# Three column parts of the layer-0 edge sums beside the experts, pauses in the column scans, two expert reloads behind the end rows

## The reference

```
x = x + gnn0(ln(x)) + mix0(ln(x))
x = x + ffn0(ln(x))       # the part that is changed
x = x + gnn1(ln(x), edges) + mix1(ln(x));  x = x + ffn1(ln(x))

ffn0: h = x @ W_gat                                  # 4 heads x 4 experts
      e = leaky_relu(a_src[src] + a_dst[dst])        # per edge and head
      alpha = softmax of e over the edges of each dst
      scores = layernorm(segment_sum(h[src]*alpha)).mean(heads); top 2, softmax -> gate
      out = sum over 4 experts: gate[e] * (gelu(x@W1[e]+b1[e]) @ W2[e] + b2[e])
```

## Time and profile before

| | |
|---|---|
| median of the runs | 4406.01 us |
| the profiled execution: its own time / its span | 4400.95 / 4399.2 us |
| busy PE, DVE, ACT, POOL | 2388.0, 1799.8, 1362.5, 1277.8 us |
| experts end / layer-1 sort begins (VectorE) | 2053.6 / 2100.4 us |
| sort ends / last sums end | 2404.6 / 2440.2 us |
| end rows there / gates begin / combine begins | 2487.2 / 2502.0 / 2516.8 us |

### The profile page before, as it was taken

How to read it: one execution, slowest core, us unless ns; L and a number is a source line. 1 busy time by engine, 2 the same in 40 slices (tenths; PEclk the granted TensorE clock), 3 DMA queues, 4 the chain that set the end, 5 groups by cost and what they waited for, 6 DMA issues and landing times. The chain is left out here.

```text
span 4399.2 us, 45890 instructions
## 1 busy us (share of the span) xinstructions
PE 2388.0 (54%) x14500; PEld 1769.9 (40%) x14500; DVE 1799.8 (41%) x3887; ACT 1362.5 (31%) x3051; POOL 1277.8 (29%) x1238
## 2 busy tenths in 40 slices
PE   3677455634111110896475126434535466899997
PEld 2532324533000110664352125333434354688885
DVE  6898355770000000113899674434434366111112
ACT  2479235631000000111268001434434332122221
POOL 0000040005777776000000215545344421500005
PEclk9999676765555555998599568667767676999998
DMA  1210112003111111111130213434333320354553
GB/s 62 93 37 0 46 32 79 0 1 60 22 13 12 9 11 11 34 33 41 60 118 39 74 36 78 156 98 149 112 126 136 97 89 21 107 188 188 186 188 93
DMA packets 165531, 322.54 MB, mean 73 GB/s; under 512 B 71298, under 2 KB 126592, under 8 KB 156845
## 3 DMA queue, kind: packets, MB, share of 16 engines
q0 software_dynamic: 62656, 149.60, 12.2%
q1 hardware_dynamic: 102753, 171.54, 11.5%
HBM read 213.40 MB, written 107.37 MB: 73 GB/s over the span
## 5 line engine op out<-in xcount | busy, mean ns | idle before, releaser
L1645 POOL DMA_INDIRECT ge_near<-gat_src,s_other x512 | 516.4, 1009 | 171.9 <-issue 171.9
L1947 PE MATMUL bank<-arena 128*125 128x256 f32 x800 | 219.9, 438 | 627.6 <-issue 582.8
L2752 POOL DMA_INDIRECT he_buf<-wh_dram,s_other x400 | 387.0, 967 | 404.3 <-DVEq L2986 283.5
L1947 PEld LDWEIGHTS bank<-arena 128*125 128x125 f32 x800 | 170.5, 218 | 683.9 <-issue 622.5
L1974 DVE TENSOR_TENSOR XN<-bank,arena 125x256 f32 (+1 forms) x100 | 42.4, 425 | 984.2 <-remote 580.1
L1960 ACT ACTIVATE arena<-bank,arena 128x500 f32<-128x500 f32 (+1 forms) x112 | 70.6, 633 | 957.8 <-DMA q_gb<-in_L_mix_bn_beta_cols 657.7
L2872 ACT ACTIVATE he_buf<-he_buf,he_e 128x128 f32<-128x128 f32 x800 | 239.4, 387 | 36.8 <-issue 34.4
L2432 ACT ACTIVATE x_hT<-bank,x_w 128x256 f32<-128x256 f32 x256 | 121.4, 474 | 379.4 <-PE bank L2384 379.4
L2393 PE MATMUL bank<-x_w,x_hT 128*128 128x256 f32 x1024 | 229.4, 382 | 6.9 <-ACT x_hT L2432 6.7
L2384 PE MATMUL bank<-x_xT,x_w 128*128 128x256 f32 x1024 | 228.1, 381 | 0.9 <-DVE x_xT L2187 0.9
L2393 PEld LDWEIGHTS bank<-x_w,x_hT 128*128 128x128 f32 x1024 | 191.9, 190 | 39.3 <-issue 13.2
(11 more groups left out here) (696 smaller groups left out, 5989.9 us busy)
## 6 DMA issues: line engine op xcount, KB each, us to landing
he_result<-he_buf SPq DMA_DIRECT2D x25, 2080.0 KB
XN<-s_a_dram SPq DMA_DIRECT2D x57, 512.0 KB
x_y<-XN SPq DMA_DIRECT2D x24, 500.0 KB
x_x<-zero SPq DMA_DIRECT2D x1, 8192.0 KB, 27.0
ge_near<-gat_src,s_other POOLq DMA_INDIRECT x512
x_xs<-x_x SPq DMA_DIRECT2D x32, 256.0 KB, 3.4
x_y<-x_ys SPq DMA_DIRECT2D x32, 256.0 KB, 2.1
he_buf<-wh_dram,s_other POOLq DMA_INDIRECT x400
```

The lines of the kernel that those rows point to most:

```text
L1645: pool.indirect_dma_start(out=G[:, c, 0:HF + H], out_offset=None, in_=m.gat_src, in_offset=bass.IndirectOffsetOnAxis(ap=ed.other[:, c:c + ...
L1947: last = pe.matmul(m.ps[4 + j % 2][:P, 0:D], self.hT[:, f, j * P:(j + 1) * P], w.w2[e][:, f, :], start=f == 0, stop=f == FC - 1)
L2752: pool.indirect_dma_start(out=buf[j][:, c, 0:HF + H], out_offset=None, in_=m.wh_dram, in_offset=bass.IndirectOffsetOnAxis(ap=ed.other[:, t ...
```

## The change

The parts become 0-128, 128-192, 192-384 and 384-512 columns. Parts 0 and 1 (192 columns) are done between the chunks of experts 2 and 3, whose loops on VectorE and ScalarE are written out; `s.spread` moves ahead of expert 2. Behind the sort come parts 2 and 3, with one `dec` of 192 columns in place of two halves of 128. The scans of both sorts are drained after every fourth. The wait for the sort and `reload(3)` leave SP's order; the small block with `reload(0)` goes; both reloads are issued by SP within `join_nodes` when the end rows have landed.

```diff
@@ Sort.vector_scan
         for i in range(KB):
             dve.tensor_tensor_scan(H3[:, 1:, i], ...)
-        dve.drain()
+            if i % 4 == 3:
+                dve.drain()
@@ join_nodes(..., then=None)
+            if then is not None:
+                @block.sync
+                def _(sp):
+                    sp.wait_ge(rows[NG - 1], 16 * GT)
+                    then(sp)
@@ gat_edges
-            dec = m.sb("ge_dec", [128, 2 * CQ, H])
+            PARTS = ((0, 128), (128, 192), (192, 384), (384, 512))
+            dec = m.sb("ge_dec", [128, 192, H])
+            dec_of = lambda q: dec[:, 0:PARTS[q][1] - PARTS[q][0], :]
@@ sync
                     s1.sync(sp)
                     sp.wait_ge(s1.negated, 1)
                     ex.reload(sp, 1)
                     ex.reload(sp, 2)
-                    sp.wait_ge(sorted1, 1)
-                    ex.reload(sp, 3)
                     keep(2)
                     keep(3)
@@ vector: logits(q) is split into scores(q) (L1665, L1667) and maxima(q) (the rest),
@@         sums(q) into weigh(q) (L1689, L1692) and sums(q, heads) (L1696)
+                    def beside(q):
+                        def between(dve, c):
+                            if c == 0:
+                                scores(q)
+                            elif c == 1:
+                                maxima(q)
+                            elif c == 2:
+                                weigh(q)
+                            elif c == 3:
+                                sums(q, (0, 1))
+                            elif c == 4:
+                                sums(q, (2, 3))
+                        return between
                     s.positions(dve)
-                    for e in range(4):
-                        ex.vector(dve, e)
+                    ex.vector(dve, 0)
+                    ex.vector(dve, 1)
                     s.spread(dve)
                     dve.drain()
-                    logits(0)
-                    logits(1)
-                    sums(0)
-                    sums(1)
+                    ex.vector(dve, 2, beside(0))
+                    ex.vector(dve, 3, beside(1))
                     dve.wait_ge(ex.freed, 4 * (NCH + 1))
                     s1.vector(dve)
-                    dve.drain().then_inc(sorted1, 1)
-                    logits(2)
-                    logits(3)
-                    sums(2)
-                    sums(3)
+                    scores(2)
+                    maxima(2)
+                    scores(3)
+                    weigh(2)
+                    sums(2, range(H))
+                    maxima(3)
+                    weigh(3)
+                    sums(3, range(H))
@@ scalar
-                    for e in range(4):
-                        ex.scalar(act, e)
-                    weights(0)
-                    weights(1)
+                    ex.scalar(act, 0)
+                    ex.scalar(act, 1)
+                    ex.scalar(act, 2, beside(0))     # weights(q) after chunk 1
+                    ex.scalar(act, 3, beside(1))
@@ end of gat_edges
-        with nc.Block() as block:
-            @block.sync
-            def _(sp):
-                sp.wait_ge(r_stored, 64)
-                ex.reload(sp, 0)
+        def reload(sp):
+            ex.reload(sp, 3)
+            ex.reload(sp, 0)
         join_nodes(..., reload)
@@ Experts0.vector and .scalar (between=None)
-        chunks(dve, body)
+        if between is None:
+            chunks(dve, body)
+        else:
+            for c in range(NCH + 1):
+                body(c, 4 if c < NCH else 1)
+                between(dve, c)
```

More of the change, by code:

```diff
@@ L1356, in _, with join_nodes @@
                 s.spread(dve)
-def join_nodes(m, tag, ed, sp_, H, F, GT, last, result, r_stored, add_nodes, own_e=None, early=None, late=None):
+def join_nodes(m, tag, ed, sp_, H, F, GT, last, result, r_stored, add_nodes, own_e=None, early=None, late=None, then=None):
     nc, cols = m.nc, ed.cols
@@ L1658, in _, with scores @@
                     mx = G[:, :, HF + H:W]
-                    def logits(q):
-                        lo, hi = q * CQ, (q + 1) * CQ
+                    def scores(q):
+                        lo, hi = PARTS[q]
                         e = spread.ke[:, lo:hi, :]
+                        blocks_done = hi // BC
                         for j in range(2):
-                            dve.wait_ge(rows[j], 16 * BC * (hi // BC // 2))
+                            dve.wait_ge(rows[j], 16 * BC * ((blocks_done + 1 - j) // 2))
                         dve.tensor_tensor(e, G[:, lo:hi, HF:HF + H], e, ALU.add)
@@ L1668, in logits, with maxima @@
                         dve.drain()
+                    def maxima(q):
+                        lo, hi = PARTS[q]
+                        e, d = spread.ke[:, lo:hi, :], dec_of(q)
                         for h in range(H):
@@ L1680, in logits, with weigh, sums @@
                         dve.drain()
-                        wide = spread.cont[:, lo:hi].unsqueeze(2).broadcast_to((128, CQ, H))
+                        wide = spread.cont[:, lo:hi].unsqueeze(2).broadcast_to((128, hi - lo, H))
                         dve.tensor_tensor(d, d, wide, ALU.mult)
                         dve.drain().then_inc(e_ready, 1)
-                    def sums(q):
-                        lo, hi = q * CQ, (q + 1) * CQ
-                        e, d = spread.ke[:, lo:hi, :], dec[:, q % 2 * CQ:(q % 2 + 1) * CQ, :]
+                    def weigh(q):
+                        lo, hi = PARTS[q]
+                        e, d = spread.ke[:, lo:hi, :], dec_of(q)
                         dve.wait_ge(e_exp, q + 1)
-                        dve.tensor_tensor(d, d, spread.cont[:, lo:hi].unsqueeze(2).broadcast_to((128, CQ, H)), ALU.mult)
+                        dve.tensor_tensor(d, d, spread.cont[:, lo:hi].unsqueeze(2).broadcast_to((128, hi - lo, H)), ALU.mult)
                         for h in range(H):
                             f = G[:, lo:hi, h * F:(h + 1) * F]
-                            dve.tensor_tensor(f, f, e[:, :, h].unsqueeze(2).broadcast_to((128, CQ, F)), ALU.mult)
+                            dve.tensor_tensor(f, f, e[:, :, h].unsqueeze(2).broadcast_to((128, hi - lo, F)), ALU.mult)
                         dve.drain()
-                        for h in range(H):
+                    def sums(q, heads):
+                        lo, hi = PARTS[q]
+                        e, d = spread.ke[:, lo:hi, :], dec_of(q)
+                        for h in heads:
                             for f in (*range(h * F, (h + 1) * F), HF + h):
@@ L1697, in sums @@
                                                        G[:, lo - 1, f:f + 1] if q else 0.0, ALU.mult, ALU.add)
[L1698 removed]
+                        if H - 1 in heads:
+                            dve.drain().then_inc(summed, 1)
+                    def beside(q):
[11 more added lines that the diff above has]
+                        return between
                     dve.tensor_copy(dst_logits[:, :, :], m.hg[:, :, 20:24])
@@ L1950, in tensor, with scalar @@
         chunks(pe, body)
-    def scalar(self, act, e):
+    def scalar(self, act, e, between=None):
         m, w, FC = self.m, self.w, self.FC
@@ L1961, in body, with vector @@
                                bias=w.b1[e][:, f:f + 1]).then_inc(self.acted, 1)
-        chunks(act, body)
-    def vector(self, dve, e):
+        if between is None:
+            chunks(act, body)
+        else:
+            for c in range(NCH + 1):
+                body(c, 4 if c < NCH else 1)
+                between(act, c)
+    def vector(self, dve, e, between=None):
         m, w = self.m, self.w
```

20 lines of the change are left out of this document (11 added, 9 removed).

## The result

Twenty runs of each kernel give 4401.58 us before and 4423.35 us after (medians; 4389.03 to 4411.55 and 4401.60 to 4430.74). The ratio of the runs is 1.0042, with an interval of 1.0030 to 1.0054: slower by a little, 21.8 us by the medians and 18.5 us by the ratio (13 to 24). The profiled execution of the changed kernel has 4424.19 us, its span 4422.5 (before 4400.95 and 4399.2). The busy times hardly differ: VectorE 1799.7 us against 1799.8, TensorE 2387.9 against 2388.0. Hardly any work was added (four table loads on ScalarE, and the pauses); what changed is what waits for what.

The account below looks back on a forecast made before the run. No engine sets the whole time; each stage has its own chain, and what ends last there counts. +13.3 from the combine on and +1.1 for layer 0's scans, +14.4 on 4404.3, gave 4419 us; own range 4412 to 4426.

Parts of the forecast that it names:

- The two reloads, the step that decides: Behind the end rows: 51.1 us for both on five engines, gates' loads queued behind them, combine 13.3 us later.
- T: Moment when the end rows are there, before gates and combine; forecast to move by -24.35 us, to 2462.8.
- Start of the sort: Layer 1's sort on VectorE: starts 29.9 us sooner, at 2070.5, bounds 2067 to 2075.
- Work between the chunks: Around experts 2 and 3: fits VectorE's idle time, but ScalarE makes TensorE late; +2.5 us, bounds 0 and twice 4.5.
- Scans: Both sorts on VectorE: seven more drains each cost +1.1 us a sort, bounds 0 and 2.
- Parts 2 and 3: Behind layer 1's sort: 320 columns in place of 256 and two new waits, +7.2 us, bounds 5 and 10.
- Start of the join: First end-row gather: without the small block's barrier it starts at about 2445.1, -2.75 us, bounds -3 and 0.
- The sum: Whole kernel: +13.3 us from the combine on and +1.1 for layer 0's sort scans, +14.4.
- Small loads pass: Rival at the gates: engines take the loads between the reloads, combine at T + 51.5, -1.4 us, 4403; 7%.
- ScalarE's tables: Rival in the sort: a table load each of six rounds, 7.7 us more, 4427; 9% together with dearer work between chunks.
- Reloads hidden: Rival at the combine: both reloads land before T + 29.65, whole -24.35 us reaches the combine, 4381; 4%.
- The base: Starting time for the whole kernel: the mean of four executions, 4404.3 us, giving 4418.7, called 4419.

Follow-up runs that it names:

- e1: Changed kernel with reload(3) issued again when the sort is over and reload(0) once the keeps have landed; 3431.71 us, ratio 0.9997 to the kernel before.
- e3: Kernel before with only the reloads of experts 3 and 0 moved behind the end rows and the small block gone; 3463.84 us, ratio 1.0097.
- e7: Changed kernel with the gates' three loads issued by SP in the join ahead of the two late reloads; 3447.03 us, ratio 1.0039 to before.
- e4: Changed kernel with every reload, still late, cut in two DMAs of 112 and 13 partitions; 3439.7 us, ratio 1.0027 to the kernel before.
- e6: Changed kernel with early reloads, reloads and first load of X cut in 112 and 13 partitions, one drain a sort; 3413.0 us, ratio 0.9943 to before.
- e8: e6 with one call moved, scores(3) behind sums(2); 3415.58 us, ratio 0.9933 to the kernel before.
- e2: Changed kernel with the gates' three loads issued by ScalarE on its own queue, reloads still late; 3462.5 us, ratio 1.0086 to the kernel before.
- c_after: The changed kernel run again, no edit, on the chips of the experiments; 3459.46 us, ratio 1.0069 to the kernel before.
- c_before: The kernel before run again, no edit, one look on the chips of the experiments; 3428.8 us.

## Why the prediction was right, point by point

- **The two reloads, the step that decides.** Forecast 51.1 us for the pair, gates at T + 52.6 and a combine at T + 67.3; measured a wait of 41.27 us, gates at T + 51.1, combine at T + 65.9. The mechanism is shown from both sides (e1, e3), and the order on the queue by the DMA view above and e7. The rule of the Trainium skill that was drawn on (DMA: Bandwidth & Descriptors, Why a DMA increments its semaphore by 16 and not by 1) holds too: 112 partitions instead of 125 filled 16 engines in e4 and e6. The price of a packet rose as more engines ran.
- **Start of the sort.** Forecast 2070.5, measured 2070.15. The 0.35 is about what the last chunk came sooner than forecast: 2.1 us late and not 2.5 (next point).
- **Work between the chunks.** Forecast +2.5 us. From chunk 1 to chunk 2 of expert 2 it is 16.23 us, as rows 1892.94 and 1909.17 show, against 14.7 for expert 3 (1986.99 to 2001.71): +1.5 and 0; 0.5 were there before the first of the new work, and the last add is 2.1 us later than before. The sort feels this in full: SP issues the keeps (2060.17) only when the last chunk's store has landed, and the sort's loads behind them. ScalarE's timeline (below) has the two Exps and the table loads at the forecast places.
- **Scans.** Forecast +1.1 us a sort, measured +1.28 and +1.7. Of layer 0's 1.7 us nothing reached the experts, whose first add came at 1065.64 against 1067.27; the forecast had added 1.1 for it.
- **Parts 2 and 3.** Forecast +7.2 us (35.4 to 42.6), measured +7.9 (35.2 to 43.1). The wait for ScalarE at 2406.41 is there.
- **Start of the join.** This term was mis-sized: forecast -2.75 us, measured -1.3. The first gather still waits 4.73 us for `keep(3)` (GpSimd's row below), and starts 6.54 us behind the last sums; I had put 5.06, from SP's reaction to `r_stored`. GpSimd is later than SP on the same semaphore: in e1 SP issues `reload(0)` at 1796.29 and GpSimd its first gather at 1797.16, 0.87 us later, and in e6 and e8 the same. The other 0.6 lie ahead of that (SP in e1 acts 5.64 us behind the last sums); why is open.
- **The sum.** Forecast +14.4 at the combine (13.3 and the 1.1 of layer 0's scans), measured +13.33. That the 13.3 came out to the digit is luck: T moved by 22.9 us and not by 24.35, and from T to the combine it is 36.2 us more and not 37.65, two errors of 1.4 that cancel. The profiled pair differs by 23.2 us as a whole, because of +10.0 behind the combine. It lies in layer 1's stage before its feed-forward part (from the combine's end 1106.4 us before, 1118.0 after), in code that is the same in both. On the other chips the stretch from the combine's end to the end was 1522.0 to 1527.9 us over ten kernels, and in the pair 1522.5 and 1522.7. Whether the change causes it on the first chip or two executions differ by chance stays open; no experiment ran there. By the ratio the whole difference is 13 to 24 us, and the forecast's +14.4 lies in that.

ScalarE and then GpSimd of the kernel after:

```profile
1890.73 1.28 ACT L1762 ACT_TABLE_LOAD   x1
1902.04 0.63 ACT L1762 ACTIVATE ge_ke<-ge_ke 128x512 f32<-128x512 f32 x1 [10.03 <-DVEq L1693]
...
1903.28 1.28 ACT L1993 ACT_TABLE_LOAD   x1
1904.57 2.38 ACT L1993 ACTIVATE arena<-bank,arena 128x500 f32<-128x500 f32 x4
```
```profile
2425.06 1.24 POOL L1403 DMA_INDIRECT ge_near<-ge_result,gj_end_i  x1 [4.73 <-DMA ge_result<-ge_near]
```

**The rivals.** *Small loads pass*: false, and e2 shows that it stays false on a queue of their own. *ScalarE's tables*: false; between 2250 and 2370 there is one load, the Exp one at 2368.25, ahead of a wait of 13.21 us. *Reloads hidden*: false, and its threshold was wrong as well. I wrote that it decides at 216 GB/s, the rate at which both land by T + 29.65. e4 had 229 GB/s and still started its combine at T + 45.2: the gates' loads stand behind the reloads, so the gates begin only when these are through, and 14.8 us follow. To be hidden they would have to be through near T + 14, at some 460 GB/s, or stand behind the gates' loads. e7 had those first and the slow rate; both together were not tried.

**The base.** The four executions at hand had a mean of 4404.3, the twenty runs a median of 4401.58. The sum on the latter would have been 4416.0; the 7.4 us that then lack are the open 10.0, less the 1.1 by which the combine came sooner than forecast (13.3 for 14.4), less the 1.5 by which the two profiled executions lie further apart (23.2) than the medians (21.8). So the forecast of 4419 is closer to the measured 4423.35 than its terms earn: a base 2.7 us too high hides part of those 7.4.

## What to carry to other kernels

A transfer that is moved behind its last cover costs its whole length, and with it the length of all that is queued behind it, however small; issue the small loads that an engine waits for before the large ones, because another queue on the same DMA engines doesn't rescue them. Look at the DMA share: 0.31 means five engines of 16, and splitting the partitions as 112 + 13 filled the others here, for a rate of 1.7 to 2.3 times and not of three. And before you move work ahead of a stage, ask which other chain ends there: on the other chips 27.5 us of a sooner sort gave under 1 us, since the last gather set when the last part could start.

## What the runs showed of the hardware

- A second queue gets one 64-byte packet through for each 25.6 KB packet of the first on the same engine (184 against 205 in 40 us), so three loads of 0.02 MB took 39 us, from 1840.9 to the gates' start at 1879.9.
- On one queue nothing of the kind happens: small loads issued behind two large ones moved no packet in 36 us (kernel after, 2476 to 2512) and all theirs in the 4 us behind. The issue of the third held SP for 23.36 us, against 0.34 with nothing in front.
- A packet of 25.6 KB takes 0.95 us with five engines at work and about 1.7 with 16: 133 GB/s became 229 (e4). Rows of 1 KB (X) went from 115 to 260 GB/s (e6).
- With a reload on five engines in flight a gather landed 10.9 us after its issue (e1); with none, 2.4 us (c_after, e6).
- A table load is 1.28 us and nothing else: the Exp before it ends at 1903.19, 1903.28 + 1.28 is 1904.56, and the Gelu starts at 1904.57. The Trainium skill (ScalarE: Activation LUTs, What ACT_TABLE_LOAD costs) has a drain of about 1.38 us besides; the measurement decides, there is none here.
- A drain between two scans costs 0.18 us (400 columns: 1.28 over 7); with 512 columns it is 1.7 over 7, 0.24, or 0.17 without the single gap of 0.48.
- The same kernel took 4401 us in the first runs and 3430 on two other occasions, on chips of its kind. Of the 654 us up to the sort of layer 1, 589 arise in expert 0, while GpSimd gathers: its 25 bias adds took 671.5 us in the first (1067.27 to 1738.78) and 82.5 in c_before (1038.64 to 1121.17). Layer 1 shows another 320 us (1842.2 against 1522.5 behind the combine). Why TensorE is held in the first runs only was not found.
